# Gene weights split into f16 parts and turned by DMA, f16 expression, a third down/up product, and a new order

## The reference

```
h = layernorm(x)
q = rope(h @ Wq); k, v = split(ctx @ Wkv); k = rope(k)          # 32 heads of 16
x = x + softmax(q k' / 4) v @ Wout + bout
h = layernorm(x);  n = h * rsqrt(mean(h * h) + eps) * norm_w
logits = n @ Wc.T / max(temperature, 0.1)                        # 1024 genes
vals, idx = top_k(logits, 32);  w = softmax(vals)
e = sum_k w_k * genes[idx_k]                                     # 64 wide
out = x + tanh(e @ Wd.T) * n * (e @ Wu.T) * scale
```

## Time and profile before

| what | us |
|---|---|
| median of 3 runs | 521.72 (521.05 to 524.21) |
| the profiled execution, its own time | 522.47 |
| span of the profile, first to last instruction | 520.6 |
| outside the span | 1.9 |
| granted TensorE clock, mean | 0.933 of full |
| POOL steps, mean: rope products, their sums | 1.28 and 1.39; 0.79 and 0.73 |
| POOL steps, mean: `split_lo`, `finish`, `add_bout`, `ln1` or `ln2` | 1.16; 1.27; 1.28; 0.55 |
| DVE steps, mean: `find_top`, `remove_top`, `group_max` | 1.23; 1.21; 1.22 |
| ACT step, mean: one `exp_group` | 1.03 |

### The profile page before, as it was taken

How to read it: one execution, slowest core, us unless ns; L and a number is a source line. 1 busy time by engine, 2 the same in 40 slices (tenths; PEclk the granted TensorE clock), 3 DMA queues, 4 the chain that set the end, 5 groups by cost and what they waited for, 6 DMA issues and landing times. The chain is left out here.

```text
span 520.6 us, 10802 instructions
## 1 busy us (share of the span) xinstructions
PE 429.7 (83%) x3744; PEld 276.6 (53%) x3744; DVE 400.8 (77%) x648; ACT 279.2 (54%) x418; POOL 263.0 (51%) x263
## 2 busy tenths in 40 slices
PE   1553777978899998999999999999989899787824
PEld 0352454545566565566666666666656566464423
DVE  5678044397889898889898989898988988878770
ACT  3425636364656666565656565656565657444220
POOL 1343726373566656475757575757575748010111
PEclk9965788989999999999999999999999999999765
DMA  6946062616172626252525252525252514111000
GB/s 213 295 99 122 13 122 33 122 22 112 34 123 53 122 54 122 52 101 72 102 71 102 70 102 70 104 69 102 72 102 52 99 46 87 39 42 19 21 21 21
DMA packets 115552, 42.92 MB, mean 82 GB/s; under 512 B 106928, under 2 KB 108992, under 8 KB 115520
## 3 DMA queue, kind: packets, MB, share of 16 engines
q1 hardware_dynamic: 114560, 41.45, 36.9%
q10 hardware_dynamic: 960, 1.05, 0.6%
HBM read 12.86 MB, written 4.19 MB: 33 GB/s over the span
## 5 line engine op out<-in xcount | busy, mean ns | idle before, releaser
L1081 PE MATMUL gene<-wcT_h,yT 128*128 128x512 f16 x256 | 83.5, 389 | 2.1 <-DMA yT<-y_hl 2.1
L915 DVE MAX8 top<-stage_b 128x8 f32<-128x1024 f32 x64 | 78.4, 1226 | 7.0 <-ACT stage_b L628 3.4
L923 DVE MATCH_REPLACE8 stage_b<-top,stage_b 128x1024 f32<-128x1024 f32 x64 | 77.5, 1211 | 0.2
L432 POOL TENSOR_TENSOR rstd<-var,minus_half 128x1 f32<-128x1 f32 x16 | 8.8, 549 | 94.0 <-DVE var L887 94.0
L392 POOL TENSOR_TENSOR x_hl<-xn,x_hl 128x512 f16<-128x512 f32 x16 | 19.5, 1219 | 71.3 <-issue 35.4
L403 POOL TENSOR_TENSOR stage_b<-stage_b,cos_t 128x512 f32<-128x512 f32 x32 | 40.8, 1275 | 18.7 <-issue 9.7
L1081 PE MATMUL gene<-wcT_l,yT 128*128 128x512 f16 x128 | 49.7, 388 | 0.0
L628 ACT ACTIVATE stage_b<-gene 128x512 f32<-128x512 f32 x32 | 18.9, 590 | 50.5 <-PE gene L1081 50.4
L404 POOL TENSOR_TENSOR stage_b<-stage_b,sin_t 128x512 f32<-128x512 f32 x32 | 44.5, 1389 | 0.0
L1191 PE MATMUL dense<-stage_a,v_ext 128*32 128x128 f32 x1024 | 40.8, 289 | 2.7 <-ACT stage_a L590 2.6
L848 DVE TENSOR_REDUCE row_max<-score_a 128x8 f32<-128x1024 f32 x32 | 39.0, 1219 | 5.1 <-PE score_a L1150 4.8
(11 more groups left out here) (158 smaller groups left out, 1027.3 us busy)
## 6 DMA issues: line engine op xcount, KB each, us to landing
x_ring<-x_dram SPq DMA_DIRECT2D x16, 256.0 KB, 3.4
out_dram<-x_ring SPq DMA_DIRECT2D x16, 256.0 KB, 2.1
ctx_sb<-ctx_dram SPq DMA_DIRECT2D x16, 128.0 KB, 2.1
stage_a<-L_ffn_Wc_dram SPq DMA_DIRECT2D x1, 2048.0 KB, 8.7
stage_b<-L_xattn_Wq_dram ACTq DMA_DIRECT2D x1, 1024.0 KB, 5.7
stage_b<-L_xattn_Wkv_dram SPq DMA_DIRECT2D x1, 1024.0 KB, 9.0
stage_b<-L_xattn_Wout_dram SPq DMA_DIRECT2D x1, 1024.0 KB, 12.0
genes_sb<-L_ffn_genes_dram SPq DMA_DIRECT2D x2, 256.0 KB, 4.9
```

What stands on the lines that cost most here:

```text
L915: nc.vector.max(top[:, 8 * n:8 * n + 8], logit if n == 0 else rest).then_inc(s_top[n], 1)
L923: nc.vector.match_replace(rest, top[:, 8 * n:8 * n + 8], logit if n == 0 else rest, REMOVED).then_inc(s_rem[n], 1)
L1081: last = nc.tensor.matmul(out, lhs(k), rhs(k), start=(n == 0), stop=(n == steps - 1))
```

## The change

The gene weights are split like the other operands. ACT writes the high f16 part of `gene_w` (`w_hi`), POOL the low part (`w_lo`), both into `w_hl`, and one transposing DMA on SP (`turn_w`) turns both. `transpose_w` and `read_wT` are gone. The genes are scaled once by a power of two and split into f16 pairs side by side (`genes_hl`, by `genes_largest`, `genes_scale`, `genes_hi`, `genes_lo`), and `express` is 16 f16 matmuls, for the two parts of the weights. `e_hi` and `e_lo` now fill 128 partitions each, and `down_up` has a third product. `negate_top` adds the logarithm of 2 to the 15, so that the weights use the range of f16.

```diff
+            def turn_w(t):
+                ready = t + 1
+                hold(sp)
+                sp.wait_ge(s_w_h, ready)
+                sp.wait_ge(s_w_l, ready)
+                if not first(t):
+                    sp.wait_ge(s_eT, t)
+                sp.dma_start_transpose(wT.rearrange("p (m t) -> p m t", t=P),
+                                       w_hl[:].rearrange("p l d -> p (l d)")).then_inc(s_wT, 16)
...
+            def w_lo(t):
+                pool.wait_ge(s_gw, t + 1)
+                pool.wait_ge(s_w_h, t + 1)
+                if not first(t):
+                    pool.wait_ge(s_wT, 16 * t)
+                pool.tensor_tensor(w_hl[:, 1], gene_w, w_hl[:, 0], ALU.subtract).then_inc(s_w_l, 1)
...
-            def read_wT(t, n):
+            def w_hi(t):
+                act.wait_ge(s_gw, t + 1)
+                if not first(t):
+                    act.wait_ge(s_wT, 16 * t)
+                nc.scalar.activation(w_hl[:, 0], gene_w, ACT.Copy).then_inc(s_w_h, 1)
...
-                nc.scalar.activation(eT_hl[:], gene[:, 0:P], ACT.Copy).then_inc(s_eT_h, 1)
+                nc.scalar.activation(eT_h[:], gene[:, 0:P], ACT.Copy, scale=w_undo[:, GENE:GENE + 1]).then_inc(s_eT_h, 1)
...
-                nc.vector.scalar_tensor_tensor(neg_top[:], top[:, 0:1], -1.0, w_undo[:, WC:WC + 1], ALU.mult,
-                                               ALU.mult).then_inc(s_ntop, 1)
+                nc.vector.scalar_tensor_tensor(neg_top[:], top[:, 0:1], w_undo[:, GENE + 1:GENE + 2], gene_w_unit[:], ALU.mult,
+                                               ALU.add).then_inc(s_ntop, 1)
...
-                nc.vector.tensor_tensor(eT_hl[GD:2 * GD], gene[GD:2 * GD, 0:P],
-                                        eT_hl[GD:2 * GD].bitcast(f32), ALU.subtract).then_inc(s_eT_l, 1)
+                nc.vector.scalar_tensor_tensor(eT_l[:], gene[:, 0:P], w_undo[:, GENE:GENE + 1], eT_h[:].bitcast(f32),
+                                               ALU.mult, ALU.subtract).then_inc(s_eT_l, 1)
...
-            def transpose_w(t, n):
+            def express(t):
+                pe.wait_ge(s_wT, 16 * (t + 1))
+                if last_tile(t):
+                    pe.wait_ge(s_tanh, t)
+                else:
+                    pe.wait_ge(s_lgr[0], t + 2)
+                if first(t):
+                    pe.wait_ge(s_split_genes, 2)
+                for g in range(2 * GK):
+                    last = nc.tensor.matmul(gene[:, 0:P], genes_hl[:, g % GK], wT[:, g * P:(g + 1) * P],
+                                            start=(g == 0), stop=(g == 2 * GK - 1))
                 last.then_inc(s_eT, 1)
...
                 cols = slice(n * DIM, (n + 1) * DIM)
-                nc.tensor.matmul(gene[:, cols], eT_hl[:], wduT_h[:, cols], start=True, stop=False)
-                nc.tensor.matmul(gene[:, cols], eT_hl[:], wduT_l[:, cols], start=False,
+                nc.tensor.matmul(gene[:, cols], eT_h[:], wduT_h[:, cols], start=True, stop=False)
+                nc.tensor.matmul(gene[:, cols], eT_h[:], wduT_l[:, cols], start=False, stop=False)
+                nc.tensor.matmul(gene[:, cols], eT_l[:], wduT_h[:, cols], start=False,
                                  stop=True).then_inc((s_dn, s_upp)[n], 1)
```

More of the change, by code:

```diff
@@ L451, in iteration @@
                     rope_sum(t3, 1)
-                    rope(t3, 0)
-                    rope_sum(t3, 0)
                     split_lo(t3, 1)
-                    add_bout(t3)
                 if t7 is not None:
                     gate(t7)
[L458 to L461, removed]
                 if later(t2):
-                    x_lo(t2)
+                    rope(t2, 0)
+                    rope_sum(t2, 0)
+                if t6 is not None:
+                    w_lo(t6)
+                if later(t1):
+                    x_lo(t1)
                 if t7 is not None:
                     finish(t7)
+                if later(t3):
+                    add_bout(t3)
+                if later(t0, 1):
+                    ln1(t0)
+                if later(t2):
+                    split_lo(t2, 0)
+                if t4 is not None:
+                    ln2(t4)
             ln1(0)
@@ L1008, in iteration @@
                 if t5 is not None:
-                    norm2_stats(t5)
-                if t4 is not None:
-                    neg_max_lo(t4)
+                    remove_top(t5, 2)
+                if t3 is not None:
+                    attn_lo(t3)
                 if t5 is not None:
-                    norm2_shift(t5)
-                if later(t2, 1):
-                    norm1_stats(t2)
+                    find_top(t5, 3)
+                    remove_top(t5, 3)
                 if t6 is not None:
-                    find_top(t6, 0)
-                    remove_top(t6, 0)
-                    find_top(t6, 1)
@@ L1020, in iteration @@
[L1020 to L1035 removed]
+                    combine(t6)
@@ L1038, in _ @@
+            run(dve, 7, iteration)
         @block.tensor
@@ L1306, in iteration @@
                 if t3 is not None:
-                    scores(t3, 0)
-                    scores(t3, 1)
+                    scores(t3, 3)
+                    scores(t3, 2)
+                if t5 is not None:
+                    logits(t5, 0)
+                if t3 is not None:
+                    transpose_max(t3)
+                if later(t2):
+                    transpose_ctx(t2)
                 if t5 is not None:
```

298 lines of the change are left out of this document (153 added, 145 removed).

## The result

The changed kernel takes 555.73 us (median of 6 runs, 554.92 to 560.42) against 521.61 in the same series: a ratio of 1.0668, 95% interval 1.0638 to 1.0699. It is slower by 34 us, and outside the predicted range. The profiled execution is the slowest of the six (560.42 us, mean granted clock 0.885, where the four fastest have 0.894 to 0.896). Its span is 558.6, where before had 520.6, so what is read from it comes out some 4 us larger than the medians have it.

A forecast was written before the change was run, and what follows sets the result against it. It held that PE leads now and DVE would decide afterwards: 23.9 of work, 0.9 and 0.2 of waits, 0.5 of collision, a 25.5 us period. With both ends the span came to 515.0, forecast 515 us, range 504 to 535.

The forecast's parts named there:

- where the new order waits: Loop: DVE waits 0.9 us around `neg_max_lo` and `ctx_lo`, 0.2 at `find_top`; `mask` collision 0.5; period 25.5.
- second and third rival: POOL's product of k delays DVE at `norm2_shift`: once, 526 us, chance 0.23; or twice, 540 us, chance 0.17.
- layout: One iteration timed from DVE's first `group_max`: `ln2` ends near 13.6 us, `read_k` near 13.4, DVE reaches `norm2_shift` at 14.0.
- the signs that would prove it wrong: Loop: `norm2_shift` or `norm1_shift` above 1 us, PE waiting for turned weights or k's turn, granted clock under 1.00.
- the third rival: POOL's products delay two of `norm2_shift`, `norm1_shift`, `negate_top`: 2.1 us per iteration, 25 in all, 540 us; chance 0.17.
- The early steps: First three periods after tile 0, as chains of latencies: 24.4, 22.5 and 24.0 us, tile 3 at 133.7.
- The collision of `mask`: DVE's `mask` meets POOL's products of q in the loop: 0.5 us charged per period, ends 0 and 1.27.
- What bounds the kernel now: Loop before the change: PE leads, busy 96%, occupied about 25.0 us of 26.02, DVE 1.1 us behind.
- DVE's floor and waits: Loop: DVE's 23.9 us of work is the period's floor; waits of 0.9 and 0.2 make 25.0.
- the sum: Span: tile 3 at 133.7, then 77.7, 153.0 and 75.3 us of periods, tail 75.3: 515.0.
- PE's and POOL's terms: Per tile: f16 `express` 1.2 us on PE, `w_lo` 2.3 on POOL; weights' turn hidden by some 1.3.
- The two ends: Start and tail: first `neg_max_hi` near 62.8 us instead of 54.0, tail 75.3 instead of 69.5.

The follow-up runs named there:

- the filler: The changed kernel plus 11 unused matmuls per tile, four ahead of `transpose_o` and seven ahead of `down_up`: 541.26 us.
- one-operand kernel: The changed kernel with `norm1_shift`, `norm2_shift` and `negate_top` taking their second operand as a scalar per row: 526.73 us, ratio 1.0076.
- e12: e11 with `y_hi` and `y_lo` earlier in the iterations behind the last tile's attention: 511.89 us, ratio 0.9793.
- e5: The one-operand kernel with DVE's `mask` moved ahead of the two `group_max` before it: 519.0 us, ratio 0.9931.
- e11: e5 with tile 0's q and k turns and scores moved earlier, and `y_lo` ahead of `normalise`: 514.63 us, ratio 0.9852.

## Why the prediction was wrong

**The step that failed is the choice between the rivals**, in the part on where the new order waits. The collision was priced for `mask` alone, at 0.5; `norm2_shift`, `norm1_shift` and `negate_top` were left free in the forecast, and went to the second and third rival with 0.23 and 0.17. The third was right in its mechanism and its place: POOL's product started 0.16 us ahead of `norm2_shift`, and the next one as the first was over. One thing differs: not the second of the three steps waited but the third. The prediction's own layout had the product ready at 13.6 and `norm2_shift` at 14.0, product first. It set that aside because in before the product came 0.13 after the step, and because a loop's end lies between `ln2` and the product. The first belonged to the phase of the old order and spoke of nothing in the new one; the second costs 0.18 (the mark at 349.49), less than the 0.4 of the layout. The runs show 0.98 and 1.09 us of held-up steps in each iteration, of which 1.2 stay in the period, where the forecast had nothing.

**Its price was mis-sized, by the clock.** The forecast had the granted clock only among the signs that would prove it wrong, and gave it no price in the loop. It costs 1.6 us per iteration of the loop, 14.5 in all. With the clock held up by the filler the time is 541, where the third rival had 540, but that nearness is luck: the filler's twelve periods behind tile 3 take 323.3, where that rival had 25 on top of the forecast's 306.0, and its tile 3 is at 141.0 instead of 133.7.

**The early steps were mis-sized too.** The forecast had 24.4, 22.5 and 24.0 for the first three periods, 70.9, and tile 3 at 133.7. After has 26.7, 26.1 and 28.5, 81.3, and tile 3 at 145.9. The one-operand kernel still needs 78.3 and e12 77.2, so most of this is neither the small steps nor `mask`; what it is stays open. Of the 43.6 us between the forecast's span of 515.0 and the measured 558.6, 33.1 lie in the twelve periods behind tile 3, 12.2 before it, and the tail gives back 1.7.

**The collision of `mask`**: 0.71 on the step and 0.59 on the period instead of 0.5, and 7.7 us over the tiles, within the ends given. The Trainium skill, "SBUF — State Buffer", section "Who interferes with whom", says that a VectorE instruction with two SBUF inputs and a GpSimd instruction that reads SBUF keep each other out for the whole length of the one that came first. The runs agree: 1.94 us with two operands under a product, 1.22 ahead of it; 1.14 and 1.24 for steps of one column with two operands, 0.20 with one.

**What bounds the kernel now** was misread. A busy share of 96% on PE was taken for the bound. With 1.6 us less of work on PE the old order kept its 26.0. PE's lighter work is no gain by itself. In the new order the period does fall, to 25.3 and 25.0, but only once DVE's steps are free (e5, e11).

**DVE's floor and waits** were nearly right: in the filler's loop 27.10 less 0.84 of waits, less 2.77 of held-up steps (`mask` 0.70, the small ones 2.07) is 23.5, predicted 23.9; the waits before `neg_max_lo` and `ctx_lo` are 0.84, predicted 0.9, and the 0.2 before the first `find_top` do not show. In e12, without these collisions, the 15 periods take 376.2 us, where the sum, with one of them at 0.5, had 376.9; that too is luck, 77.2 instead of 70.9 in the first three and 299.0 instead of 306.0 in the other twelve.

**PE's and POOL's terms**: `express` 1.07 (1.2), `w_lo` 2.12 (2.3), the turn of the weights hidden in the loop, as predicted.

**The two ends**: the first `neg_max_hi` at 64.6 (62.8), the tail 73.6 (75.3): both near, and with opposite signs.

## What to carry to other kernels

Where steps of two engines keep each other out, look where the small steps of one fall under the long ones of the other: here a step of 0.15 us took 1.14 to 1.24 behind a product of 1.28, and the profile books that as busy, not as waiting. Give such steps their second operand as a scalar per row where that can be. Before a busy share is called a bound, ask what happens to the period if that engine gets lighter: here 1.6 us of PE's work per tile could go and nothing moved. By the traces the period hangs on closed chains through several engines, and only work inside such a chain counts; that is argued here, not tested.

## What was not expected of the hardware

In after PE stands 1.2 to 1.3 us and, eight transposes later, 1.6 to 1.8 in twelve iterations. Behind that the granted clock fell to its lower level in eight of them, for 3.4 to 6.1 us, and not in the other four, whose gaps are as long. With the second gap gone (the one-operand kernel, which keeps 1.18 there and has 0.85 elsewhere), or with both filled, it stayed at 1.00 in the loop. After a gap of 2.83 us in e11 it fell too; after one of 2.84 at the same place in e12 it did not. What decides it, these runs do not show.
